# The last eleven dense blocks of a four-layer graph network: kept in a table and merged behind the scatters, with a stretch in which no dense block begins

## The reference

```
x = layernorm(x + L0(x, edge_attr, src, dst))   # edge softmax over dst, messages summed at dst, + bias
x = layernorm(x + L1(x, ...))                   # edge softmax over dst; then gelu, layernorm, MLP, layernorm per node
x = layernorm(x + L2(x, ...))                   # degree-normalised messages, summed at src, @ W.T + b
x = layernorm(x + L3(x, ...))                   # edge_weight * x[dst], summed at src
```

## Time and profile before

| | |
|---|---|
| median of 3 runs | 2841.71 us (2838.56 to 2847.09) |
| the profiled execution | 2843.06 us, its span 2841.0 us |
| PE busy | 1953.7 us (69%) |
| DVE busy | 1671.3 us (59%) |
| ACT busy | 1500.6 us (53%) |
| POOL busy | 1661.1 us (58%) |
| memory traffic | 203.19 MB, mean 72 GB/s |

### The profile page before, as it was taken

How to read it: one execution, slowest core, us unless ns; L and a number is a source line. 1 busy time by engine, 2 the same in 40 slices (tenths; PEclk the granted TensorE clock), 3 DMA queues, 4 the chain that set the end, 5 groups by cost and what they waited for, 6 DMA issues and landing times. The chain is left out here.

```text
span 2841.0 us, 27494 instructions
## 1 busy us (share of the span) xinstructions
PE 1953.7 (69%) x8422; PEld 1016.5 (36%) x8422; DVE 1671.3 (59%) x3188; ACT 1500.6 (53%) x2243; POOL 1661.1 (58%) x1609
## 2 busy tenths in 40 slices
PE   6998787779988788898999867568988863000000
PEld 3444333227643343374444345443343342000000
DVE  4876699983888778735565426987565784000000
ACT  3787566562777678737777733357777721000000
POOL 6777777500037663003777577765777067777777
PEclk9999899786998889979999976569899955555555
DMA  2223222111647763113444653432112231000000
GB/s 63 69 65 82 54 59 67 44 38 56 201 99 50 45 51 36 48 30 99 135 135 137 160 145 86 122 96 63 53 51 58 80 111 58 15 16 20 22 21 21
DMA packets 219591, 203.19 MB, mean 72 GB/s; under 512 B 144815, under 2 KB 157958, under 8 KB 219446
## 3 DMA queue, kind: packets, MB, share of 16 engines
q1 hardware_dynamic: 164998, 154.80, 19.3%
q0 software_dynamic: 51200, 46.31, 11.7%
q10 hardware_dynamic: 3248, 0.34, 0.1%
HBM read 134.59 MB, written 80.28 MB: 76 GB/s over the span
## 5 line engine op out<-in xcount | busy, mean ns | idle before, releaser
L2320 POOL DMA_INDIRECT stab<-wk,rank_i x200 | 209.3, 1046 | 295.1 <-DVE wk L580 236.7
L537 ACT ACTIVATE b_s<-ps,vec 128x512 f32<-128x512 f32 (+1 forms) x356 | 241.1, 684 | 176.4 <-PE ps L616 63.3
L2317 POOL DMA_INDIRECT u<-x2tab,dpos_i x200 | 223.8, 1119 | 79.8 <-issue 74.9
L2317 POOL DMA_INDIRECT u<-x3tab,src_i x200 | 206.6, 1033 | 88.9 <-issue 58.9
L2317 POOL DMA_INDIRECT e_b<-x0tab,dpos_i x72 | 71.4, 991 | 301.6 <-DVEq L2122 270.6
L2317 POOL DMA_INDIRECT u<-in_x_dram,src_i x200 | 201.7, 1009 | 76.2 <-issue 59.0
L2317 POOL DMA_INDIRECT u<-in_x_dram,dst_i x200 | 201.5, 1008 | 64.2 <-issue 59.7
L2320 POOL DMA_INDIRECT out_dram<-u,sfin_i x200 | 196.5, 982 | 66.4 <-issue 66.4
L2320 POOL DMA_INDIRECT out_dram<-u,dst_i x176 | 187.0, 1062 | 56.3 <-issue 56.3
L545 ACT ACTIVATE b_gl<-ps,vec 128x1024 f32<-128x1024 f32 (+1 forms) x148 | 163.3, 1107 | 70.9 <-PE ps L521 69.3
L531 PE MATMUL ps<-b_s,blk_j 128*128 128x512 f32 (+1 forms) x296 | 163.0, 635 | 51.0 <-ACT b_s L550 50.5
(11 more groups left out here) (419 smaller groups left out, 4934.2 us busy)
## 6 DMA issues: line engine op xcount, KB each, us to landing
b_gl<-in_x_dram SPq DMA_DIRECT2D x98, 256.0 KB, 2.7
out_dram<-b_gl SPq DMA_DIRECT2D x98, 256.0 KB
wk<-dlist SPq DMA_DIRECT2D x50, 500.0 KB
wk<-slist SPq DMA_DIRECT2D x50, 500.0 KB
u<-stab SPq DMA_DIRECT2D x25, 510.0 KB
x2none<-b_gl SPq DMA_DIRECT2D x25, 250.0 KB
wk<-x2none SPq DMA_DIRECT2D x25, 240.0 KB
x2tab<-wk SPq DMA_DIRECT2D x25, 240.0 KB
```

The costliest lines, as they stand in the source:

```text
L537: return nc.scalar.activation(b_s[l][:, 0:w], pB[l][:, 0:w], ACT.Abs_reciprocal_sqrt, bias=col(EPSV))
L2317: pool.indirect_dma_start(out=o, out_offset=None, in_=tab, in_offset=at(ix), **kw).then_inc(s, 16)
L2320: pool.indirect_dma_start(out=tab, out_offset=at(ix), in_=a, in_offset=None, bounds_check=rows_n - 1, oob_is_err=False).then_inc(s, 16)
```

## The change

1. The first 87 dense blocks are stored to `out` as before; the last 11 (LATE) are stored to a table of their own in memory, `late_tab`.
2. While POOL is in its third phase ("u3"), SP fills the rows of those 11 blocks in `out` with a marker, 3e38, from a 128x64 tile: 11 DMAs of 256 KB.
3. Before its 400 scatters POOL waits for the stores of the first 87 blocks and for the 11 marker fills, no longer for blocks 87 to 97.
4. Behind the last scatter SP loads the rows of the 11 blocks from `out`, DVE merges them with the table's rows (where the marker still stands, the dense row; else the scattered row) in three instructions per block, and SP stores them. The table's rows are loaded into `wk` ahead of this.
5. `HOLD` has an entry: no dense block takes a lane between group 20 of the third phase and the third destination block (`dst` 2). All dense blocks have rank 2.
6. One semaphore is saved by letting `consts` stand for `cleared` as well.

```diff
+    LATE = 11
+    LATE0 = NBLK - LATE
+    UNSET = 3e38
...
+    late_tab = dram("late_tab", (LATE * NB, D))
...
+        unset = sb("unset", [128, D])
+        late_d = w_[0:LATE]
+        late_o = [b_gl[k % NL][:, 512 * (k // NL):512 * (k // NL) + 512] for k in range(2 * NL)] + b_h + b_s
+        late_m = b_x1[0][:, 0:GC * LATE]
...
-                 ([(("dense", NBLK - 1 - k), "out", STORED) for k in range(NL)] if p == 0 else []))
+                 ([(("dense", LATE0 - 1 - k), "out", STORED) for k in range(NL)] if p == 0 else []))
         for n in range(NBLK):
...
-        HOLD = ()
+        HOLD = ((("u3", 20, "t"), ("dst", 2, "t")),)
...
-            if n == NBLK - 1:
-                lp, mp, _ = place["dense", n - 1]
-                sp.wait_ge(S(f"rows_st{lp}"), 16 * before(lp, mp + 1, dense=1, src=1))
-            sp.dma_start(out[dense_row(n):dense_row(n) + NB, :].rearrange("(p t) d -> p (t d)", p=128),
-                         b_gl[l][:, 0:512]).then_inc(S(f"rows_st{l}"), 16)
+            tab, row = (out, dense_row(n)) if n < LATE0 else (late_tab, NB * (n - LATE0))
+            sp.dma_start(tab[row:row + NB, :].rearrange("(p t) d -> p (t d)", p=128), b_gl[l][:, 0:512]).then_inc(S(f"rows_st{l}"), 16)
+
+        FIRST_FOUND = 6
+        LATE_LOADS = [LATE - 1, LATE - 2] + list(range(LATE - 2))
+        LATE_STORES = [LATE - 2] + list(range(LATE - 2)) + [LATE - 1]
+
+        def late_rows(j):
+            return out[dense_row(LATE0 + j):dense_row(LATE0 + j) + NB, :].rearrange("(p t) d -> p t d", p=128)
+
+        def unset_sp(sp, t, j):
+            yield t
+            sp.wait_ge(S("pool_c"), 6)
+            if j == LATE - 1:
+                sp.wait_ge(S("late_dma"), 16 * (LATE - 1))
+            sp.dma_start(late_rows(j), unset[:, :].unsqueeze(1).broadcast_to((128, GC, D))).then_inc(S("late_dma"), 16)
+
+        def late_sp(sp, t):
+            yield t
+            sp.wait_ge(S("summed"), 4 * NG)
+            for l in LANES:
+                sp.wait_ge(S(f"rows_st{l}"), 16 * before(l, len(lane_jobs[l]), dense=1, src=1))
+            sp.wait_ge(S("late_dma"), 16 * LATE)
+            for j in range(LATE):
+                sp.dma_start(late_d[j], late_tab[NB * j:NB * j + NB, :].rearrange("(p t) d -> p (t d)", p=128)).then_inc(S("late_dma"), 16)
+            sp.wait_ge(S("final_st"), 256 * NG)
+            for k, j in enumerate(LATE_LOADS):
+                sp.dma_start(t3(late_o[j]), late_rows(j)).then_inc(S(f"late_found{int(k >= FIRST_FOUND)}"), 16)
+            sp.wait_ge(S("late_found0"), 16 * FIRST_FOUND)
+            for k, j in enumerate(LATE_STORES):
+                sp.wait_ge(S("late_step"), 3 * k + 3)
+                if k == LATE - 1:
+                    sp.wait_ge(S("late_dma"), 32 * LATE + 16 * k)
+                sp.dma_start(late_rows(j), t3(late_o[j])).then_inc(S("late_dma"), 16)
+            sp.wait_ge(S("late_dma"), 48 * LATE)
+
+        def late_dve(dve, t):
+            yield t
+            dve.wait_ge(S("late_dma"), 32 * LATE)
+            for k, j in enumerate(LATE_STORES):
+                m, d, o = late_m[:, GC * j:GC * j + GC], t3(late_d[j]), t3(late_o[j])
+                second = LATE_LOADS.index(j) >= FIRST_FOUND
+                dve.wait_ge(S(f"late_found{int(second)}"), 16 * (LATE - FIRST_FOUND if second else FIRST_FOUND))
+                nc.vector.tensor_scalar(m, o[:, :, 0], UNSET / 2, UNSET, ALU.is_lt, ALU.mult).then_inc(S("late_step"), 1)
+                dve.wait_ge(S("late_step"), 3 * k + 1)
+                nc.vector.tensor_tensor(d, d, bc(m, D), ALU.add).then_inc(S("late_step"), 1)
+                dve.wait_ge(S("late_step"), 3 * k + 2)
+                nc.vector.tensor_tensor(o, o, d, ALU.min).then_inc(S("late_step"), 1)
+
...
+            sp_programs += [unset_sp(sp, at["u3", 0]["t"] + 20 * j, j) for j in range(LATE)]
+            sp_programs += [late_sp(sp, 1e6)]
             play(*sp_programs)
-            for l in LANES:
-                sp.wait_ge(S(f"rows_st{l}"), 16 * before(l, len(lane_jobs[l]), dense=1, src=1))
-            sp.wait_ge(S("final_st"), 256 * NG)
...
+            nc.gpsimd.memset(unset[:, :], UNSET).then_inc(S("pool_c"), 1)
...
             for l in LANES:
-                pool.wait_ge(S(f"rows_st{l}"), 16 * before(l, len(lane_jobs[l]), dense=1, src=1))
+                early = max(m for m, (_, kind, n) in enumerate(lane_jobs[l]) if kind == "dense" and n < LATE0)
+                pool.wait_ge(S(f"rows_st{l}"), 16 * before(l, early + 1, dense=1, src=1))
+            pool.wait_ge(S("late_dma"), 16 * LATE)
             for kind, g in FINAL:
...
+            dve_programs += [late_dve(dve, 1e6)]
```

More of the change, by code:

```diff
@@ L304, in gnn_resnorm_kernel @@
             unit(("final", p), 0, "t pool 10.6", [(("final", p - 1) if p else ("u6", NG - 1), "t", 0), step] +
-                 ([(("dense", NBLK - 1 - k), "out", STORED) for k in range(NL)] if p == 0 else []))
+                 ([(("dense", LATE0 - 1 - k), "out", STORED) for k in range(NL)] if p == 0 else []))
         for n in range(NBLK):
-            unit(("dense", n), 1 if n >= 80 else 2, "t pe .68 +lane;u act|dve .7;c pe 1.13;sq act .6;j pe 1.13;r act 1.27;h dve 1.35;" + (ROW_MLP if n >= BY_ROWS else MLP),
+            unit(("dense", n), 2, "t pe .68 +lane;u act|dve .7;c pe 1.13;sq act .6;j pe 1.13;r act 1.27;h dve 1.35;" + (ROW_MLP if n >= BY_ROWS else MLP),
                  [(("dense", n - 1), "t", 0)] if n else ())
@@ L1648, in index_sp @@
             yield 1
-            sp.wait_ge(S("cleared"), 1)
+            sp.wait_ge(S("consts"), 1)
             full = E // 256
@@ L2182, in setup_loads @@
         def setup_loads(act):
-            act.wait_ge(S("cleared"), 1)
+            act.wait_ge(S("consts"), 1)
             n = 0
@@ L2213, in setup_pe @@
             pe.wait_ge(S("loaded"), LOADED)
-            pe.wait_ge(S("consts"), 1)
+            pe.wait_ge(S("consts"), 2)
             nc.tensor.transpose(pA[0][:, 0:128], wbd[:, 0, :], ident[:, :])
@@ L2310, in _, with at_ix @@
                            allow_small_or_imprecise_dtypes=True).then_inc(S("pool_c"), 1)
-            def at(ap):
+            nc.gpsimd.memset(unset[:, :], UNSET).then_inc(S("pool_c"), 1)
+            def at_ix(ap):
                 return bass.IndirectOffsetOnAxis(ap=ap, axis=0)
@@ L2316, in gather @@
                 kw = {} if rows_n is None else dict(bounds_check=rows_n - 1, oob_is_err=False)
-                pool.indirect_dma_start(out=o, out_offset=None, in_=tab, in_offset=at(ix), **kw).then_inc(s, 16)
+                pool.indirect_dma_start(out=o, out_offset=None, in_=tab, in_offset=at_ix(ix), **kw).then_inc(s, 16)
             def scatter(tab, rows_n, ix, a, s):
-                pool.indirect_dma_start(out=tab, out_offset=at(ix), in_=a, in_offset=None, bounds_check=rows_n - 1,
+                pool.indirect_dma_start(out=tab, out_offset=at_ix(ix), in_=a, in_offset=None, bounds_check=rows_n - 1,
                                         oob_is_err=False).then_inc(s, 16)
@@ L2431, in _ @@
                 nc.vector.memset(a[96:128, :], int(SKIP))
-            dve.drain().then_inc(S("cleared"), 1)
+            dve.drain().then_inc(S("consts"), 1)
             nc.vector.memset(ones, 1.0)
```

## The result

The changed kernel takes **2817.79 us**, the median of 20 runs (2794.24 to 2844.31). The kernel before, run 20 times beside it, takes 2828.41 (2813.06 to 2847.09), so the median of three shown ahead of the prediction, 2841.71, lay high. The ratio is 0.9946, with a 95% interval of 0.9927 to 0.9966: the change is faster by 0.54%, about 15 us. The ratio leaves out the two slowest runs of the changed kernel, which lie over 1.5% above its fastest; the medians of all runs are 10.6 us apart. The prediction said 2819, faster, by 0.8%. The time is met and so is the sign. That part is luck.

A forecast was written before the change was run, and what follows sets the result against it. POOL's wait for dense stores before its first scatter was taken to bound the kernel. First scatter -61, scatters +16, tail +22.4 put the span 22.8 us lower: 2819 us beside a median of 2841.71, forecast 2806 to 2832, range 2798 to 2843.

The forecast's parts named there:

- What bounds the kernel: End of kernel: only POOL's scatters are busy, so an earlier first scatter brings the end forward one for one.
- The wait that goes: Before the first scatter: POOL waits for 87 blocks, not 98; block 86 stored at 2223, first scatter 2228, 61 us earlier.
- by its place: Block 86's store, estimated from the store in that position of SP's order before: 2220.19 + 10 = 2230.
- the count of blocks: Block 86's store, estimated from four blocks less to make up behind the hold: 2157.57 + 50 + 10 = 2218.
- The hold: Softmax to destination groups: gain up to 25 us, price up to 25, nearly cancelling; later work shifts by +10 us.
- the second rival: Destination groups carry two blocks in full: shift 23, first scatter 2248, 2839, no change; 35 or more, slower; chance 0.20.
- The clock: Held softmax stretch: TensorE's lower clock slows only transposes there and the first destination block's; 0 to 5 us, inside +10.
- Slower scatters: The 400 scatters: all 25 `main3` groups and the late blocks run beside them, losing 40 us against 24, +16.
- The full lock: Scatters beside `main3`: two-SBUF-input DVE instructions block POOL entirely, loss 96 us instead of 40, 2875 us; chance 0.05.
- The tail: Behind the last scatter: loads, eleven merges and stores take 27.7 us instead of 5.3, +22.4.
- The fills: POOL's third phase of gathers: eleven marker fills, 2.75 MB, are covered by some 1200 us and cost nothing.
- The own row of the fourth group: Behind the first scatters: POOL waits for the fourth group's own row instead, costing 5 us, 2824; chance 0.05.

The follow-up runs named there:

- run 20: Not a label but part of "run 20 times": the kernel before, unaltered, measured 20 times beside the changed kernel, median 2828.41 us.
- hold-alone kernel: The kernel before with only the HOLD entry added, no late table and no merge: 2894.9 us, ratio 1.0222.
- the repeat: The changed kernel run and profiled once more, unaltered: 2815.01 us, ratio 0.9933 to the kernel before.

## Why the prediction was right, and where it wasn't

**What bounds the kernel**: right. The time of the first scatter carried over to the end nearly one for one. In the hold-alone kernel it moves by +56.6 us and the span by +52, the rest being scatters that lost less.

**The wait that goes**: off by 11 us. Block 86 was stored at 2236.5, where I had taken 2223 between 2207 and 2243. The estimate "by its place", 2220.19 plus the shift, gives 2240 with the shift as it was, within 4. Going by the count of blocks was the poorer choice, for two reasons. The shift in it was 10 and measured 20. And the hold is not all that moves block 86: without it 91 stores stand ahead of `carried`, not 92, and block 86 is stored 34 us ahead of the last gather's end (2179.42 and 2213.4) where it was 45. About one block's pitch comes from the rest of the edit, which I had put at nothing that can be seen; the dense blocks' rank is the likely part, not tried alone. Landing and release took 2.9 us, not 5.0. That the store would still be what POOL waits for, and by about 15 us, was right: 16.6 and 11.9.

**The hold**: the step that failed, as "Gain and price nearly cancel ... I take +10". The gain was 26.3 us, just above my upper bound of 25. The price was 38.8, far above its bound of 25. The bound counted the two blocks' own work and no more. Their matmuls are some 20 us of PE; what was left out is that the other matmuls of the stage run slower (about 7 us) and that PE idles for 11 us more. POOL's waits between record groups come to 53.5 us, with single ones of 18.0, where they were 16.3 and 2.8. That the 11 us come from destination blocks and dense blocks sharing the three lanes is argued, not tried. The shift of the last gather's end was 20, with the longer third phase in it. That is the start of the second rival ("The hold costs more than it pays"), whose harmless half asked for 23.

**The clock** inside that term. TensorE's granted clock is 0.50, its lower level of 1.2 GHz, all through the held softmax, with PE busy 5.75 of 23.2 us, where it was 0.94 with dense matmuls between. The softmax is 6.0 us shorter for all that, so the low level costs less there than the dense work did. The price shows behind it. The block sums take 43.0 us at 0.50 throughout, against 38.5 at a mean of 0.56; their 200 matmuls take 42.8 us in all seven profiles with a hold, and 38.4 to 41.3 in the seven without. I had put 0 to 5 us on the clock, and said that only transposes could be slower; 1.5 to 4.4 us went to the block sums, which I had called unaffected, and about 7 to the record stage at 0.96. The Trainium skill, TensorE: Matmul & The Clock Gate, Part 1, says that throttled is the default and that activity releases the throttle. The trace agrees in that the clock fell to 0.50 when the dense matmuls left and stayed there; but the stretch, which by that rule alone would have been slower, was 26.3 us shorter.

**Slower scatters**: +5 instead of +16. Busy time above 0.982 each came to 27.4 us where I had 40 (36 for 25 groups at 1.45, and 4). It was 24.2 before for 16.5 groups; with 25 groups and the late blocks it is 1.1 a group at most. My step "1.45 us lost per group" took the loss to go with the number of groups. It may go with how the runs of two-SBUF instructions lie on DVE: `main3` is stretched now, with 6.9 us between own rows (2272.2 to 2417.1 for 22) instead of 5.5, and dense instructions that read PSUM between. That this stretching is the cause is argued from the timeline, not tried. The full lock (2875) did not come about: it asked for 96 us, and 27.4 were found.

**The tail**: right. SP issues the first load 1.2 us behind the last scatter, and the timeline of the tail shows the rest:

```profile
2792.08 0.81 SPq L760 DMA_DIRECT2D b_s<-out_dram  x2
...
2799.26 0.17 DVE L776 TENSOR_SCALAR b_x<-b_s 128x8 f32<-128x8 f32 x1 [371.74 <-DMA b_gl<-out_dram]
2799.46 0.69 DVE L778 TENSOR_TENSOR wk<-wk,b_x 128x512 f32<-128x512 f32 x1
...
2816.82 0.33 SPq L766 DMA_DIRECT2D out_dram<-b_s  x1
```

The loads took 7.2 us to the first merge (4.8 forecast), the eleven merges 17.0 at 1.53 (17.6 at 1.6), and last store and end 3.1 (4.3): 28.4 against 27.7. The mis-sized part is the landing: the last of the first six loads was issued by about 2794.8 and landed some 4.4 us later, where I had 2.7.

**The fills**, "their cover is some 1200 us", with a cost of nothing: off by some 10 us in their stage, with the cover there. In the kernel nothing in that phase waits for them; which resource they share with the gathers isn't shown, and no kernel separates the effect on the end.

**The own row of the fourth group** as a rival: right in mechanism. It is worth 0.3 us in the first profile of the change, where the store hides it, and 4.9 in the repeat, near the 5 forecast for it. Without the hold it is 8.1 us:

```profile
POOL out_dram L2372 <- DVE u L1628: 8.7, 3, 8.1
```

One small reading was off without changing the sum: 283 us for 25 groups of records are 11.4 a group, not 11.8, since the stretch ends with the last group's own eight scatters.

So the forecast held by luck in its size: the hold cost 11 us more than I thought and the scatters 11 less. That the wait was what bounded the kernel, and what the tail costs, was no luck.

**Open**: why single executions of one kernel differ by up to 1.8% (2794 to 2844 us for the changed one), what the fills cost at the end, and the 13.6 us between the medians of 11 and 8 late blocks. The rank of the last dense blocks was changed along with the rest and never tried alone.

## What to carry to other kernels

When filler work is held back to let a latency-bound stretch run faster, price it where it starts again: behind the hold it meets the next stage's own work on the busiest engine and in the same buffers, and here it cost 39 us for 26 gained. It also pushes all later filler back, and so a wait for filler at the end. Moving the last filler blocks behind a long stage of pure transfers pays as long as the merge it needs (1.5 us a block here) is shorter than the work taken off the wait (12.5 a block), and only until that wait is gone; here eight blocks were enough for that. A forecast that meets the total can still rest on wrong terms, so compare it term by term, on two profiles of each kernel.

## What the runs showed of the hardware that I had not expected

- One indirect scatter on POOL, 0.98 us alone, took 4.35 us beside five back-to-back DVE instructions with both inputs in SBUF; an instruction of the same size with one input in PSUM cost less than half as much (9 against 22 us for 25 of them, one profile each).
- 200 matmuls of 8 columns kept PE busy for 42.81 of 43.0 us, and the granted clock stayed at 0.50 throughout. Entered behind dense matmuls at a higher clock they took 38.4 to 41.3 us (seven profiles), and the clock fell to 0.50 under them: 0.74 in the first 10 us of the kernel before, 0.50 in the next.
- Eleven fills of 256 KB from one small tile, issued in 0.55 us each, went with a stage of 200 random gathers that was some 10 us longer (five profiles against nine); in two other such stages they made no such difference.
- POOL pauses for about 3.0 us (2.96 to 3.03) after 113, 226 and 339 of the 400 scatters, in all 14 profiles; only the first of the three was longer in five of them, 3.45 to 5.28 us.
